# The end of a round, re-planned: a phase without attention takes a chain of each stream, and one closing chain moves behind the barrier

## Time and profile before

| | us |
|---|---|
| median of 3 runs | 2313.88 |
| the profiled execution, its device time | 2315.39 |
| its span, first to last instruction | 2313.5 |
| mean granted TensorE clock (share of 2.4 GHz) | 0.92 |
| PE busy | 1852.8 (80%) |
| VectorE busy | 1335.2 (58%) |
| ScalarE busy | 1205.2 (52%) |
| GpSimd busy | 365.3 (16%) |

### The profile page before, as it was taken

One profiled execution on the slowest core, in us unless ns is written; L12 is line 12 of the kernel. 1 busy time (PEld: TensorE's weight loads), 2 busy tenths in 40 slices (PEclk: granted clock), 3 DMA queues, 4 the chain that ended last, 5 costly groups with the idle time before them and its releaser, 6 DMA issues.

```text
span 2313.5 us, 40668 instructions
## 1 busy us (share of the span) xinstructions
PE 1852.8 (80%) x13184; PEld 1406.7 (61%) x13184; DVE 1335.2 (58%) x3255; ACT 1205.2 (52%) x2794; POOL 365.3 (16%) x835
## 2 busy tenths in 40 slices
PE   1889886787689988777768998777768899877777
PEld 1677665554477766555557776555546776665554
DVE  2667565763267756576226765666624675656742
ACT  1556443457355654355645555345655565543565
POOL 0000003421100001332200000233210000023321
PEclk7999998999799999898979999989888999998999
DMA  5000000000000000000000000000000000000000
GB/s 131 7 1 1 1 1 1 1 1 1 18 1 1 1 1 1 1 2 1 1 18 1 1 1 1 1 1 1 1 9 9 1 1 1 1 1 1 1 1 6
DMA packets 23858, 13.68 MB, mean 6 GB/s; under 512 B 9202, under 2 KB 23157, under 8 KB 23637
## 3 DMA queue, kind: packets, MB, share of 16 engines
q1 hardware_dynamic: 23636, 10.92, 1.9%
HBM read 9.86 MB, written 1.05 MB: 5 GB/s over the span
## 4 chain that ended last, share of the span: by engine, by line
PE 59%; DVE 22%; ACT 9%; issue 5%; DMA 2%; POOL 1%; SPq 1%; POOLq 0%; ACTq 0%; DVEq 0%
PE heads_out L922 9%; DVE nmax L1678 6%; PE turned L545 5%; PE chain_bank L605 4%; PE heads_out L861 3%; PE scores L475 3%; PE scores L477 3%; PE scores L476 3%; PE chain_bank L545 3%; PE turned L848 3%; PE heads_out L545 2%; PE scores L827 2%; PE chain_bank L475 2%; PE queries_m L475 2%; ACT L1064 2%
## 5 line engine op out<-in xcount | busy, mean ns | idle before, releaser
L1678 DVE TENSOR_REDUCE nmax<-scores 128x1 f32<-128x512 f32 (+1 forms) x768 | 517.3, 685 | 155.4 <-PE scores L477 76.0
L1204 ACT ACTIVATE probs<-scores,nmax 128x256 f32<-128x256 f32 (+1 forms) x512 | 292.9, 577 | 43.1 <-DVE nmax L1678 42.3
L1220 ACT ACTIVATE probs_t<-turned 128x512 f32<-128x512 f32 x384 | 219.9, 597 | 121.1 <-PE turned L848 114.9
L922 PE MATMUL heads_out<-probs_t,v 128*64 128x256 f32 (+1 forms) x2560 | 266.1, 402 | 3.2 <-ACT probs_t L1230 3.2
L1805 POOL TENSOR_TENSOR rstd<-var_eps,minus_half 128x2 f32<-128x2 f32 x80 | 58.1, 726 | 1261.1 <-DVE var_eps L1349 1213.5
L545 PE MATMUL turned<-ident,probs 128*128 128x128 f32 x1536 | 239.5, 279 | 5.1 <-ACT probs L1204 4.6
L545 PEld LDWEIGHTS turned<-ident,probs 128*128 128x128 f32 x1536 | 192.9, 145 | 46.2 <-ACT probs L1204 11.1
L1880 POOL CAST q_mask<-q_t 32x256 fp32r<-32x256 f32 x384 | 159.8, 416 | 287.6 <-DVE q_t L1402 89.4
L848 PE MATMUL turned<-shifted_mask,k_t 128*128 128x256 f32 x768 | 177.2, 321 | 26.7 <-ACT probs_t L1220 22.1
L827 PE MATMUL scores<-k_t,q_mask 128*128 128x256 f32 (+1 forms) x512 | 173.5, 396 | 24.8 <-DVE nmax L1678 12.2
L1005 ACT ACTIVATE t_hi<-queries_m 128x256 fp32r<-128x256 f32 (+1 forms) x256 | 98.0, 383 | 176.1 <-PE queries_m L477 175.1
(11 more groups left out here) (333 smaller groups left out, 3997.5 us busy)
## 6 DMA issues: line engine op xcount, KB each, us to landing
out_t<-ctx_dram SPq DMA_DIRECT2D x8, 192.0 KB, 2.7
v<-wqt_dram SPq DMA_DIRECT2D x2, 512.0 KB
wo<-wo_dram SPq DMA_DIRECT2D x2, 512.0 KB, 5.3
x<-x_dram SPq DMA_DIRECT2D x8, 128.0 KB, 2.6
y_dram<-x SPq DMA_DIRECT2D x8, 128.0 KB, 2.3
v<-wkt_dram SPq DMA_DIRECT2D x1, 512.0 KB
probs_t<-wv_dram SPq DMA_DIRECT2D x1, 512.0 KB
wff<-wff_dram SPq DMA_DIRECT2D x1, 512.0 KB, 6.7
```

The lines of the kernel that those rows point to most:

```text
L922: last = nc.tensor.matmul(O[rows, 0:S], stationary, probs_t[:, h % ph.slots, kb, :], start=(kb == 0), stop=(kb == ph.kb - 1))
L1204: last = nc.scalar.activation(out, src, ACT.Exp, bias=nmax[:, h * QB + qb:h * QB + qb + 1], accum_out=sums[:, qb, h:h + 1])
L1220: nc.scalar.activation(half_probs[:, v % ph.halves, :, :], bank[:, :].rearrange("p (k q) -> p k q", k=2), ACT.Exp).then_inc(sem["attention ...
L1678: nc.vector.tensor_reduce(out, src, AX.X, ALU.max, negate=True).then_inc(sem["attention_max"], 1)
```

## The change

Five things, all by tables or by which buffer a step uses:

1. In phase `l3` of stream 0, `mid3` of stream 1 is cut in two (`CUTS`): only its steps up to `hat` stay there, spread over the whole phase, and the first step of the next `start` of stream 0 (`ctx`) joins at unit 0.
2. A new phase without attention, of 48 units (`BETWEEN`), follows: lane one is `end` of stream 0 and the rest of `start` of stream 0, lane two the rest of `mid3` of stream 1. Ordered by due unit: t0, m3_t, t1, down, nat_t, kt2, squares, wo, kt3, rmshat, stats, rms_t, hat, rsplit, q, ln1, qrope, split, root, v0, unit, high, v1, low, v2, qt0, v3, qt1.
3. Phase `l3` of stream 1 has no chain beside it, and the round ends behind it.
4. `end` of stream 1 moves into `self0` of stream 0 of the next round, ahead of `start` of stream 1 (units 0, 0, 0 and 1 of 16, then `ctx` at 2 and `stats` at 3, where both were at 0). For it there are a segment `second` (round one, without such an `end`), two loop passes instead of three, and a segment `over` with the last `end` alone.
5. SP loads ctx of stream 0's next batch as soon as the turned queries of `mid3` of stream 0 are made; the store of y and the load of x of stream 0 follow `end` of stream 0 in the new phase. Stream 1's store and load of x now fall into the next round's `self0`. A second set of scratch tiles (`Scratch`) serves `end` and `start` of stream 0; it lies partly in `probs`, idle at that time. The `HELD` rule of the planner changes no order in the other phases. In `end` of stream 1, t1 now goes through the same PSUM bank as t0.

```diff
-PAIR = [... ("l3", 0, [[("mid3", 1)]])]
+def large(before):
+    return [("self0", 0, [before + [("start", 1)]]), ("self0", 1, [[("mid0", 0)]]), ("cross0", 0, [[("mid0", 1)]]),
+            ("cross0", 1, [[("mid1", 0)]])]
+def small(chain, behind):
...
+            ("l3", 0, [[("mid3", 1, 0)]] + chain),
+            ("", 0, [[("end", 0)] + behind, [("mid3", 1, 1)]]),
+            ("l3", 1, [])]
 SEGMENTS = {
-    "first": [("", 0, [[("start", 0)]])],
-    "loop": PAIR + [("l3", 1, [[("end", 0), ("start", 0)]]), ("", 0, [[("end", 1)]])],
-    "last": PAIR + [("l3", 1, [[("end", 0)]]), ("", 0, [[("end", 1)]])],
+    "first": [("", 0, [[("start", 0, 0), ("start", 0, 1)]])],
+    "second": large([]) + small([[("start", 0, 0)]], [("start", 0, 1)]),
+    "loop": large([("end", 1)]) + small([[("start", 0, 0)]], [("start", 0, 1)]),
+    "last": large([("end", 1)]) + small([], []),
+    "over": [("", 0, [[("end", 1)]])],
 }
-LOOPS = B // STREAMS - 1
+LOOPS = B // STREAMS - 2
+CUTS = {("mid3", 1): ("m3_t",), ("start", 0): ("stats",)}
+SECOND_SCRATCH = {("end", 0), ("start", 0)}
+HELD = ("x1_t", "text", "s0", "s1", "pv")
+BETWEEN = 48
...
+    if (chain, s) in (("mid1", 0), ("end", 1)):
+        return "chain"
...
-    ("start", 1): {"ctx": 0.8, "stats": 4, ...},
+    ("start", 1): {"ctx": 2, "stats": 4, ...},
+    ("end", 1): {"t0": 0.6, "t1": 0.6, "nat_t": 0.6, "wo": 1.5},
...
             eng.wait_ge(segments_over, ends)
+            if isinstance(ends, int):
+                eng.drain()
...
+            def next_first(b):
+                for content in ("qt0", "qt1"):
+                    sp.wait_ge(sem[filled(("mid3", 0, content))], FILL["mid3", 0, content])
+                load_ctx(0, b + STREAMS)
+                store(0, b)
+                load_x(0, b + STREAMS)
...
             with sp.Fori(0, LOOPS) as b:
                 enter("loop")
-                load(1, b * STREAMS + 1)
-                store(0, b * STREAMS)
-                load(0, b * STREAMS + 2)
+                load_ctx(1, b * STREAMS + 3)
                 store(1, b * STREAMS + 1)
+                load_x(1, b * STREAMS + 3)
+                next_first(b * STREAMS + 2)
                 segment_over()
```

More of the change, by code:

```diff
@@ L207, in bank_name @@
         spare = s == 0 and content in ("v1", "v3")
-    return "spare" if spare and (chain, s) != ("mid1", 0) else "chain"
+    return "spare" if spare else "chain"
 def filled(key):
@@ L222, in due, with steps_of @@
     return [(int(sum(pace[:n]) * units / sum(pace)), step) for n, step in enumerate(steps)]
+def steps_of(name, s, part=None):
+    steps = STEPS[name].split()
+    if part is None:
+        return steps
+    bounds = [0] + [steps.index(cut) for cut in CUTS[name, s]] + [len(steps)]
+    return steps[bounds[part]:bounds[part + 1]]
 def planned(lanes, units):
     steps = []
-    for lane in lanes:
-        steps += due([(name, s, step) for name, s in lane for step in STEPS[name].split()], units)
-    return sorted(steps, key=lambda at: at[0])
+    for n, lane in enumerate(lanes):
+        steps += [(at, n, step) for at, step in
+                  due([(*item[0:2], step) for item in lane for step in steps_of(*item)], units)]
+    waiting, plan = sorted(steps, key=lambda at: at[0]), []
+    while waiting:
+        held = plan and plan[-1][2][2] in HELD
+        at, lane, step = waiting.pop(next(k for k, w in enumerate(waiting) if not held or w[1] == plan[-1][1]))
+        plan.append((max(at, plan[-1][0] if plan else 0), lane, step))
+    return [(at, step) for at, _, step in plan]
 def enter(segment):
@@ L248, in enter @@
             ORDER.append((phase, ps))
-        PLAN.append(planned(lanes, PHASES[phase, ps].steps if phase else 1))
+        PLAN.append(planned(lanes, PHASES[phase, ps].steps if phase else BETWEEN))
         for lane in lanes:
-            ORDER.extend(lane)
+            ORDER.extend(item[0:2] for item in lane if item[2:] in ((), (0,)))
         for _, (chain, s, step) in PLAN[-1]:
@@ L304, in run_rounds @@
     ending = iter(())
+    work, ahead = {}, {}
     for (phase, ps, lanes), plan in zip(SEGMENTS[segment], PLAN):
[L306 to L310, removed]
+        units = PHASES[phase, ps].steps if phase else BETWEEN
+        for lane in lanes:
+            for name, s, *part in lane:
+                if part in ([], [0]):
+                    work[name, s] = chain(name, s)
+                    ahead[name, s] = next(work[name, s], None)
+        emitted = attention(PHASES[phase, ps]) if phase else iter((None,) * (BETWEEN + 1))
         next(emitted)
@@ L320, in run_rounds @@
                 at += 1
-        assert not any(ahead.values())
         ending = emitted
     assert next(ending, "over") == "over"
+    assert not any(ahead.values())
 def program(nc, A, y_out):
@@ L584, in turn_heads @@
                     for g in range(QUADS):
-                        if qb == 0:
+                        if qb == 0 and precedes((phase, s), (chain, s)):
                             pe.wait_ge(sem["attention_out_scaled"], PHASES[phase, s].at("out_scaled", g + 1))
@@ L996, in _ @@
             segment("first", 1)
+            segment("second", 2)
             with pe.Fori(0, LOOPS) as b:
-                segment("loop", b + 2)
-            segment("last", LOOPS + 2)
+                segment("loop", b + 3)
+            segment("last", LOOPS + 3)
+            segment("over", LOOPS + 4)
         @block.scalar
```

97 lines of the change are left out of this document (61 added, 36 removed), and 5 rows, old and new, of tables (PACE, PAIR).

## The result

The changed kernel takes **2349.1 us**, the median of four runs (2345.95 to 2353.62), against 2313.3 (2309.29 to 2314.91) for the kernel before in the same comparison: a ratio of 1.0159, 95% interval 1.0134 to 1.0184. The direction was forecast, the size was not: 22 us above the forecast of 2327, and 7 us beyond the upper end of the range.

The account below looks back on a forecast made before the run. No single engine was the bound; time went where small dependent steps follow each other. Looped rounds +20.3, last round +3.3, boundaries -7.5, jump -3.9, over +0.9 gave +13.1 on 2313.9: 2327 us, range 2298 to 2342.

Parts of the forecast that it names:

- l3 of stream 0, 26.5 in the loop: l3 of stream 0 with the light chain: 26.5 us per looped round (24.5 to 27.5), 24.4 in the last.
- ctx was put at 2.1: In l3 of stream 0, ctx's copy on ACT ahead of the second exponential delays it: +2.1 us.
- The base of 23.4: Starting value for l3 of stream 0: 23.4 us, from the last round's l3 with four chain steps.
- The phase, 34.0 in the loop: New phase without attention, C of stream 0 to E of stream 1: 34.0 us looped (30.5 to 36.5), 23.6 last.
- Rival 1: New phase: the two chains fill each other, phase 30.5 us; -16 us in all, 2298 us; chance 0.25.
- l3 of stream 1, 23.8: l3 of stream 1 without a chain: 22.3 us bare plus 1.5 for a low-clock start; 23.3 in the last round.
- Boundaries and the jump, -7.5 and -3.9: Round boundaries: end of stream 1 behind the barrier, -2.5 us three times, -7.5; one backward jump fewer, -3.9.
- taken at 3.0: Start of self0: end of stream 1 added there costs 3.0 us (bounds 1.5 and 4.5).
- The segment over, +0.9: Program's end: segment over puts a barrier and a fresh t0 ahead of the last end, +0.9 us.
- The untouched phases, 0: Rest of each round: the change was taken to touch only the round's end, so no term here.
- Rival 3: From x's arrival on, all at 1.2 GHz, and end in self0 4.5 us: +32, 2344 us; chance 0.13.

Follow-up runs that it names:

- stats late: The changed kernel with one pace line added, so stats of start of stream 0 is due after root of mid3; 2326.2 us, ratio 1.0044.
- the phase alone: The changed kernel with end of stream 1 kept at the round's end, three loops, old segments and old ctx due time; 2356.9 us, ratio 1.0176.
- ctx in the phase: The changed kernel with the ctx step of start moved from l3 of stream 0 into the phase without attention; 2342.7 us in one execution.
- start beside l3: The changed kernel with the second part of start of stream 0 (stats onward) beside l3 of stream 1; 2328.1 us, ratio 1.0047.
- the version with end moved: The kernel before with only end of stream 1 moved behind the barrier into the next self0, plus two extra segments; 2304.5 us, ratio 0.9943.

## Why the prediction was wrong

**The mechanism was right.** DVE waits for x ahead of stats, mid3 stands behind it, and the phase is the loss: taken alone it costs 40 us, and with stats late it takes 1.4 us less per looped round than the better level of the full change, 4.35 less than the level with the same clock, and l3 another 2. End of stream 1 behind the barrier and one jump fewer are gains. What was off are sizes, 23.8 us in the profile (36.9 against 13.1):

- **l3 of stream 0, 26.5 in the loop: 26.86.** The sum fits by two errors that cancel. ctx was put at 2.1 for the late second exponential. It is late, as forecast: 2.89 us behind E0 instead of 0.92. But without ctx the phase takes 26.15 to 26.8, so that lateness is absorbed. The base of 23.4, taken from an l3 with four chain steps, was too low for one with eight: in the last round, where ctx is missing and nothing cancels, I said 24.4 and it took 26.47. These 2.1 us, half of the last round's miss, are hardly the clock's: in round one the same l3 ran at 1.00 throughout and took 26.86.
- **The phase, 34.0 in the loop: 33.70, 33.88 and 36.67.** In the sum again a hit at one level. Its parts were not: store and load took 1.83 and 2.11 us, 4.0 with their issue and not 5.3, and the store began at +10.75 and not +11.8, so DVE waited 3.6 us and not 5; x came at +14.7 and not +16.9. Rival 1 named just that, 4 us for both, and gave 30.5; but what follows x ran at 1.2 GHz for the most part and took 19.0 us where I had 17.1: 9.2 of it from unit to E1, where I took 7.6. The level of 36.7, where the clock falls 3 us behind C0, was in no step of mine except as a bound. In the 15 such phases of five profiles (three of the full change, the phase alone, ctx in the phase) it stands seven times, at +3 us; with stats late and with start beside l3 the early fall stands in all nine looped rounds. The last round: 24.6 against 23.6.
- **l3 of stream 1, 23.8: 24.8 to 25.0**, last round 24.5 against 23.3. Bare and at the high clock it takes 22.8 (22.3 forecast), so the low clock at its start costs 2.1 and not 1.5.
- These three make +26.5 and not +20.3 in the loop, and +7.6 and not +3.3 in the last round.
- **Boundaries and the jump, -7.5 and -3.9: -10.7.** Right in the sum. The parts differ: C1 to the first matmul takes 0.95 us instead of 10.4 or 6.4. What end of stream 1 then costs in self0 was taken at 3.0. From the first matmul to the fourth copy the kernel before took 32.35 us, the full change 35.9 and the version with end moved 32.25. The clocks tell how to read this:

```profile
630.30:662.67 32.37, 28.51 (x193) 24.61 (x194) 20.33 (x51) 19.33 (x65) 0.70 (x1) 0.83 0.01 3
```

```profile
632.06:667.97 35.91, 30.76 (x207) 26.22 (x208) 21.95 (x55) 19.72 (x66) 0.69 (x1) 0.86 0.05 14
```

```profile
617.43:649.70 32.27, 26.80 (x207) 22.37 (x208) 21.59 (x56) 19.49 (x66) 0.70 (x1) 1.00 0.06 16
```

  At about the same clock (0.83 before, 0.86 in the full change) end costs 3.6. The version with end moved (third row) has the same instructions as the full change at 1.00, and its clock pays this back; the chain is not free there. The full change had the 36.9 in all six boundaries without the jump in its three profiles; the version with end moved had 33.2 in three of its four. The loop's backward jump shows as 3.70 us of issue instead of 4.20, and entering the loop shows no such price (36.86 and 36.93 us to the fourth copy with and without it).
- **The segment over, +0.9: +2.1.** After the last C1 the end of the closing chain ran at the low clock, with 1.20 us for wo's four matmuls (2346.32), which took 0.68 in the phase of round one (582.00).
- **The untouched phases, 0: +11.0** in this pair of profiles, 6.4 in the mean of three of each. That was no term of the sum at all; I costed the middle of the round at nothing and named no work that would keep its clock.

The step that failed is the price of TensorE's clock. It was given 1.5 us in l3 and a share of the bounds in the phase, and nothing outside the round's end. In its place the runs show the middle of the round longer by 6.4 us in the mean (11.0 in the first pair), in step with the time at the 1.2 GHz level; the phase at 36.7 us instead of 33.7 in 7 of 15 rounds; and 2.1 us in each l3 of stream 1, where I had 1.5. Cross2 of stream 0, at 1.00 in the trace of before, I took as given, and the middle as a whole, at 0.94 there, too. The other misses are sizes: the base of l3 of stream 0 (2.1 us in the last round). Why the full change has more time at the low level in the middle than the kernel before stays open. Rival 3, with a chance of 0.13 and 2344 us (by its own terms, 2313.9 and 32, it is 2346), had the right cause, but none of it in the first half of the phase or outside the round's end. The range left its upper part out, and had no term at all for the rest of the round.

The Trainium skill, TensorE: Matmul & The Clock Gate, section HAM oscillation, says that waits between bursts make each burst start cold. Its case is a long wait for a DMA ahead of each burst, and there the trace agrees: PE stood idle 6.9 us around the wait for x, and the clock halved (0.88, then 0.50). In the phase's first 11 us, where PE's waits for the other engines were under 1 us each, the clock stayed at 1.00 in round one and fell to 0.50 in round three, with the same instructions; this the section does not foretell.

One reading of the prediction needs a word. The activation 0.02 us behind the table load is the helper's own first one (at 554.25), which the earlier trace rows does not show; the scaling of mid3 follows 0.13 us behind the load. In the changed kernel the load at 577.94 began 0.01 us after the end of the activation ahead of it, so nothing but the load's own 1.28 us shows there either.

What showed as announced: DVE's wait ended by the DMA of x; the second exponential 2 us late; C1 to the first matmul about 1 us, and 4.35 where the loop jumps; 24 to 25 us of phase in the last round. What did not: 0.50 "in the second half of the phase" was 13 us from x's arrival on, with 1.00 again ahead of E1 and 0.50 behind it.

## What to carry to other kernels

A closing chain of small dependent steps cost 3.6 us inside the next dense phase, behind a barrier, at a comparable clock, and 5.7, its store included, where nothing ran beside it; so move such chains to dense work one by one, and don't gather them in a stretch of their own: start's steps beside those of mid3 still cost 5.6 us there (32.3 against 26.7) when no wait stood in their way. In such a stretch look at what stands first in an engine's order: one wait for a transfer, ahead of steps that were ready, cost 1.4 to 4.35 us per round here, and a changed due time took it away. And where a change thins out TensorE's work, price its clock as a term of its own, there and in the first microseconds of what follows.

## What the hardware showed that I had not expected

- **Equal instructions at several fixed lengths.** The second half of cross0 of stream 1 took 40.7, 41.9 or 45.0 us, self2 of stream 0 61.0 or 64.1, cross2 of stream 0 46.2 or 48.7 (each a few times between); within a level they agree to 0.3 us. The two of cross2 differ by the granted clock, 1.00 and 0.93.
- **The start of self0 at two levels of the clock**, from the same code behind the barrier. The version with end moved took 33.2 us to its fourth output copy, the full change 36.9. Their second windows of 4 us behind C1 (616.45 and 631.11), and the fourth of the full change:

```profile
620.45:624.45 4.00, 2.89 (x22) 2.66 (x22) 2.20 (x6) 2.19 (x9) 0.00 (x0) 1.00 0.01 4
```

```profile
635.11:639.11 4.00, 3.07 (x13) 2.75 (x13) 1.81 (x3) 1.41 (x5) 0.00 (x0) 0.50 0.00 0
...
643.11:647.11 4.00, 2.96 (x15) 2.76 (x16) 1.10 (x4) 1.29 (x5) 0.00 (x0) 0.70 0.00 0
```

  In the second window PE is busy about as long in both, with 22 matmul records in the one and 13 in the other. What decides between the two, and whether the l3 before the barrier does, no run here settles.
- **A profile's span can lie well off its kernel's median**: the version with end moved had spans of 2291.5 and 2309.8, and runs from 2293 to 2321. Where two versions differ by 5 us, parts of the timeline at equal clock tell more than one execution's total.
